# Two small elementwise operations of an attention stage move from VectorE to GpSimd

## The chip, the cores and the metric

The kernel runs on 1 core of one Trainium2 chip. The metric is the device time of one execution in microseconds (us), as the median of several runs. The profiled execution has a span as well, from its first to its last instruction; all rows below are read from that one execution.

## The reference

One transformer block on x of shape (2, 2048, 512), in float32, conditioned by a vector per batch. What matters here is the attention, with 16 heads of width 32 and 2048 keys:

```python
attn = jnp.einsum('bhqd,bhkd->bhqk', q, k) * (1.0 / np.sqrt(hd))
attn = jax.nn.softmax(attn, axis=-1)
out = jnp.einsum('bhqk,bhkd->bhqd', attn, v)
out = out.transpose(0, 2, 1, 3).reshape(B, T, C)
return out @ w_ao + b_ao
```

Before it come the conditioning, a normalisation and the projection to q, k and v with rotation; after it the output projection, a second normalisation and a gated feed-forward layer.

## The kernel before

The kernel is a sequence of stages: `stage_p` (conditioning), `stage_a` (q, k, v), `stage_b` (attention), `stage_c` (output projection and second normalisation) and `stage_d`, called twice (feed-forward). Only `stage_b` is touched. It lies between about 500 us and 2480 us of the span.

**Units.** Attention is done in 32 units (`UNITS`). A unit is a group of 4 heads (`GH`) of one batch and a block of 512 queries (`TB`); each group of heads has 4 units, and the first of them (`j % 4 == 0`) also sets off the load of the keys and values of the next group (`load_group`, 4 MB). They are called the loading units here. Within a unit `kt` runs over 16 tiles of 128 keys. The index u of the code counts so that the output work of unit u - 1 is done while unit u is computed.

**One step of kt.** TensorE works through a written-out order: `ORDER[kt]` says where the score matmuls (`s`, L805), the matmuls for the row maxima of a later unit (`m`, L780), the denominator matmuls (`d`, L810) and the transposition of the maxima (`t`, L799) stand. The order of a plain step is "smsdmmsms", of which the `d` is taken only at kt 0, 2 and 13, and it is followed by four matmuls of probabilities by values (L870, recorded as eight), here called the PV block. At kt 12 the order is "smsdmsmst". ScalarE takes the exponential of each of the four score tiles (L651) into one of four slots of the ring `pt`. VectorE reduces each of the four `m` tiles to a maximum (L714). A score matmul waits until the exponential two tiles earlier is done (`LEAD = 2`), an `m` matmul until the reduction four tiles earlier is done (`EARLY = 4`). Each engine works strictly in the order of its own program, and waits with its semaphores where it stands.

**Denominators.** The probabilities are added over kt. GpSimd adds the tiles of `BY_POOL` (kt 0, 1, 2, 4, 5, 7, 8, 10, 11, 13, 14; ten additions L686 of 128x2048), sends those of `BY_DMA` (kt 3, 6, 9) into `side` by accumulating DMAs (L693, L697), and adds `side` itself after kt 11 (L701, `SIDE_AT`). The rest goes to TensorE. Before ScalarE writes a slot of the ring again, `slot_free` waits until the adder of its old tile is done with it. The sums are ready when GpSimd has done its last addition (kt 14), and TensorE needs them at kt 2 of the next unit.

**The output of the unit before.** ScalarE copies the products (`read_products`, L623, after two exponentials of kt 0) and the denominators (`read_denominators`, L627, after kt 2) to memory that all can read. SyncE spreads the denominators over the partitions by DMAs, VectorE inverts them (`invert`, L728, at kt 4), and four DMAs bring the reciprocals back as `r_sb`. Then come the three steps around the change:

- `divide`, L732: `on` = `o_sb` * `r_sb`, 128x512, on VectorE after its reductions of kt 8
- `round_output`, L632: `o_hi` = `on` rounded, on ScalarE after its exponentials of kt 9; it waits for `on_ready`
- `split_output`, L736: `o_lo` = `on` - `o_hi`, on VectorE after its reductions of kt 10; it waits for `ohi_ready`

SyncE stores both (`store_output`, L571), and only behind them in its queue come the maxima of the next unit (`load_maxima`, L564 and L566), which TensorE needs for the first score of the next unit, issued in kt 15. `read_products` of the next unit waits for `olo_ready` too. The instruction that holds ScalarE's place is

```python
def round_output(u):
    act.wait_ge(on_ready, u + 1)
    act.wait_ge(o_stored, 32 * (u + 1))
    act.activation(o_hi[:], on[:], ACT.Copy).then_inc(ohi_ready, 1)
```

The functions in full, with the line numbers of the profile:

Of the kernel before, what the change touches and what calls it, by code (L numbers as in the profile page):

```python
# [17 lines left out]
ALU = mybir.AluOpType  # L18
# [11 lines left out]
GH = P // HD  # L30
NG = NB * H // GH
NK = T // P
UNITS = NG * NJ
# [9 lines left out]
def f32(ap):  # L43
    return ap.bitcast(F32)
# [431 lines left out]
def stage_b(nc, io, keep, scratch):  # L476
# [9 lines left out]
    with ExitStack() as stack:  # L486
# [15 lines left out]
        o_sb, d_sb, r_sb, on = (m.sb(n, [P, TB]) for n in ("o_sb", "d_sb", "r_sb", "on"))  # L502
        dcol = m.sb("dcol", [P, GH * TB // P])
        o_hi, o_lo = m.sb("o_hi", [P, TB], F32R), m.sb("o_lo", [P, TB], F32R)
# [22 lines left out]
        def added(kt):  # L527

            return max(BY_POOL.index(kt), 1) + (kt > SIDE_AT)
# [11 lines left out]
        def run(eng, body):  # L541
            with eng.Fori(0, UNITS // 8) as pair:
                for j in range(8):
                    body(8 * pair + j, pair, j)
# [120 lines left out]
        @block.gpsimd  # L665
        def _(pool):
            pool.memset(one_rows, 1.0).then_inc(ones_ready, 1)

            pool.memset(acc[1][:], 1.0).then_inc(ones_ready, 1)
            pool.wait_ge(ones_in, 32)  # L670
            pool.memset(pt[:, RING - 1, :, :], 1.0).then_inc(ones_ready, 1)
            pool.sem_inc(pool_added, NPOOL)

            def body(u, pair, j):
                sums = acc[j % 2]
                for kt in range(1, NK):
                    if kt in BY_POOL:
                        n = added(kt) - 1
                        pool.wait_ge(p_ready, STEPS * (u + 1) + GH * (kt + 1))
                        if n == 0:  # L680
                            pool.wait_ge(d_ps, u + 1)
                            a = pt[:, BY_POOL[0] % RING, :, :]
                        else:
                            pool.wait_ge(pool_added, NPOOL * (u + 1) + n)
                            a = sums[:]
                        pool.tensor_tensor(sums[:], a, pt[:, kt % RING, :, :], ALU.add).then_inc(pool_added, 1)  # L686
                    elif kt in BY_DMA:
                        n = BY_DMA.index(kt)
                        pool.wait_ge(p_ready, STEPS * (u + 1) + GH * (kt + 1))
                        if n == 0:  # L690
                            pool.wait_ge(pool_added, NPOOL * (u + 1) + added(kt - 1))
                            pool.nop(nofuse=True)
                            pool.dma_start(side[:], pt[:, kt % RING, :, :]).then_inc(side_in, 16)  # L693
                        else:
                            pool.wait_ge(side_in, 16 * (len(BY_DMA) * u + n))
                            pool.nop(nofuse=True)
                            pool.dma_start(side[:], pt[:, kt % RING, :, :], accum_op=ALU.add).then_inc(side_in, 16)  # L697
                    if kt == SIDE_AT:
                        pool.wait_ge(side_in, 16 * len(BY_DMA) * (u + 1))
                        pool.wait_ge(pool_added, NPOOL * (u + 1) + added(kt))  # L700
                        pool.tensor_tensor(sums[:], sums[:], side[:], ALU.add).then_inc(pool_added, 1)  # L701

            run(pool, body)

        @block.vector
        def _(dve):
            dve.sem_inc(max_done, ITEMS)
            dve.sem_inc(olo_ready, 1)
            dve.sem_inc(mlo_ready, 1)

            def maxima(n, slot, lo, hi):
                for i in range(lo, hi):
                    dve.wait_ge(max_ps, ITEMS * n + i + 1)
                    dve.tensor_reduce(mpart[slot][:, i // 4, i % 4:i % 4 + 1], ps_m[:, i % EARLY, :], AX.X, ALU.max).then_inc(max_done, 1)  # L714

            def finish_max(n, slot):
                dve.wait_ge(max_done, ITEMS * (n + 2))
                dve.tensor_reduce(mneg[:], mpart[slot][:], AX.X, ALU.max, negate=True).then_inc(mneg_ready, 1)

            def split_max(n):  # L720
                dve.wait_ge(mT_ps, n + 1)
                dve.tensor_copy(m_hi[:], ps_m[0:GH * SUB, EARLY - 1, 0:P]).then_inc(mhi_ready, 1)
                dve.wait_ge(mhi_ready, n + 1)
                dve.tensor_tensor(m_lo[:], ps_m[0:GH * SUB, EARLY - 1, 0:P], f32(m_hi[:]), ALU.subtract).then_inc(mlo_ready, 1)

            def invert(u):
                dve.wait_ge(dcol_in, 16 * (u + 1))
                dve.reciprocal(dcol[:], dcol[:]).then_inc(recip, 1)  # L728

            def divide(u):  # L730
                dve.wait_ge(r_in, 16 * GH * (u + 1))
                dve.tensor_tensor(on[:], o_sb[:], r_sb[:], ALU.mult).then_inc(on_ready, 1)  # L732

            def split_output(u):
                dve.wait_ge(ohi_ready, u + 1)
                dve.tensor_tensor(o_lo[:], on[:], f32(o_hi[:]), ALU.subtract).then_inc(olo_ready, 1)  # L736

            maxima(0, 0, 0, ITEMS)
            finish_max(0, 0)
            maxima(1, 1, 0, PLAN[TURN])  # L740
            split_max(0)
            maxima(1, 1, PLAN[TURN], AHEAD)

            def body(u, pair, j):
                at = AHEAD
                for kt in range(NK):
                    if kt == TURN:
                        finish_max(u + 1, (j + 1) % 2)
                        at = 0
                    ahead = 1 if kt < TURN else 2  # L750
                    maxima(u + ahead, (j + ahead) % 2, at, at + PLAN[kt])
                    at += PLAN[kt]
                    if kt == TURN:
                        split_max(u + 1)
                    if kt == 4:
                        invert(u)
                    if kt == 8:
                        divide(u)
                    if kt == 10:
                        split_output(u)  # L760

            run(dve, body)
            invert(UNITS)
            divide(UNITS)
            split_output(UNITS)

        @block.tensor
        def _(pe):
# [502 lines left out]
def build(nc, io, out):  # L1271

    scratch = {}
    for name, shape in (("qk_hi", (2, NG, P, T)), ("qk_lo", (2, NG, P, T)), ("v", (NG, P, NK, P)), ("o_hi", (NG, P, T)),
                        ("o_lo", (NG, P, T)), ("h_hi", (NG, P, T)), ("h_lo", (NG, P, T)), ("y0", (NB, T, D)),
                        ("y1", (NB, T, D)), ("m", (2, 2, GH * TB)), ("d", (2, GH, TB))):
        scratch[name] = nc.dram_tensor(f"scratch_{name}", shape, F32, kind="Internal").ap()
    with ExitStack() as whole:
        m = Memory(nc, whole, "keep")
        keep = {"chan": m.sb("chan", [P, C_ALL]), "cond_ab": m.sb("cond_ab", [P, NB, 4, KT]),  # L1280
                "ident": m.sb("ident", [P, P]), "ones": m.sb("ones", [P, P]),
                "bao": m.sb("bao", [P, D]), "bfo": m.sb("bfo", [P, D]),
                "w_ao": m.sb("w_ao", [P, KT, D])}
        with ExitStack() as early:
            m = Memory(nc, early, "early")
            keep |= {"w_hi": m.sb("w_hi", [P, KT, 3 * D], F32R), "w_lo": m.sb("w_lo", [P, KT, 3 * D], F32R),
                     "cos": m.sb("cos", [P, T]), "sin": m.sb("sin", [P, T]), "bv": m.sb("bv", [P, D]),
                     "x": m.sb("x", [P, SUB, D])}
            stage_p(nc, io, keep)
            stage_a(nc, io, keep, scratch)  # L1290
        nc.disable_value_cache = True
        stage_b(nc, io, keep, scratch)
        nc.disable_value_cache = False
        stage_c(nc, io, keep, scratch)
        for half in range(2):
            stage_d(nc, io, keep, scratch, out, half)
# [37 lines left out]
```

## Time and profile before

| | |
|---|---|
| median of 3 runs | 3795.44 us (3787.93 to 3796.56) |
| the profiled execution, its own time | 3794.34 us |
| its span | 3792.4 us |
| TensorE matmul busy, share of the span | 3380.3 us, 89% |
| VectorE busy | 2198.2 us, 58% |
| ScalarE busy | 1592.5 us, 42% |
| GpSimd busy | 1929.7 us, 51% |

PE is TensorE, DVE is VectorE, ACT is ScalarE, POOL is GpSimd and SP is SyncE. The shares are averages over stages with different limits: GpSimd's lies almost all in `stage_b`. An engine's row in a timeline gives start, duration, line, operation, output and inputs, count, and in square brackets how long the engine sat idle before it and what ended the wait. Several instructions in a row are merged into one row with a count.

### The profile page before, as it was taken

To read this page: it belongs to the slowest core of one execution; us is meant where nothing else is said; L and a number is where in the kernel's file an instruction comes from. 1 tells how busy PE (TensorE), PEld (TensorE's weight loads), DVE (VectorE), ACT (ScalarE), POOL (GpSimd) and SP (SyncE) were. 2 spreads that over 40 slices of the span, in tenths; PEclk is the share of its full clock that TensorE was granted. 3 is DMA by queue.
4 is the path that set the end of the run, shared out by engine and by line. 5 is a ranking of instruction groups with operands and counts; after the bars stand their busy time and mean duration, and the time that the engine had idled before them with its cause. 6 is when DMAs were issued, how large, how long until landed. Compare 5 with 4: busy or idle time off the path is not lost. (4 is left out here: it accounts for less than half of the span.)

```text
span 3792.4 us, 53992 instructions
## 1 busy us (share of the span) xinstructions
PE 3380.3 (89%) x15699; PEld 2105.7 (56%) x15699; DVE 2198.2 (58%) x3311; ACT 1592.5 (42%) x2851; POOL 1929.7 (51%) x634
## 2 busy tenths in 40 slices
PE   6888689999899998998989989956499999799999
PEld 5666444444344443443434444445388888688887
DVE  2878577877688786787777877835322222322212
ACT  1343136656566565565656656623311111211111
POOL 0222248988799898888888888944200000100000
PEclk9999779999999999998999999977699999899999
DMA  4444532343533434334334352367422120331120
GB/s 173 141 141 141 140 95 74 92 117 77 122 77 93 113 85 116 83 84 116 86 87 114 74 135 73 80 235 245 141 97 89 44 86 14 122 106 49 59 74 23
DMA packets 168123, 389.98 MB, mean 103 GB/s; under 512 B 23946, under 2 KB 41466, under 8 KB 150142
## 3 DMA queue, kind: packets, MB, share of 16 engines
q1 hardware_dynamic: 139700, 250.89, 22.4%
q0 software_dynamic: 17664, 113.26, 12.1%
q10 hardware_dynamic: 10512, 22.81, 1.8%
q8 instruction: 122, 2.00, 0.2%
q14 instruction: 125, 1.02, 0.1%
HBM read 183.83 MB, written 102.27 MB: 75 GB/s over the span
## 5 line engine op out<-in xcount | busy, mean ns | idle before, releaser
L714 DVE TENSOR_REDUCE b_mpart<-b_m 128x1 f32<-128x512 f32 x2127 | 1326.8, 683 | 416.1 <-PE b_m L780 415.0
L651 ACT ACTIVATE b_pt<-b_s 128x512 f32<-128x512 f32 x2048 | 1123.7, 595 | 775.5 <-PE b_s L805 723.1
L686 POOL TENSOR_TENSOR b_acc<-b_acc,b_pt 128x2048 f32<-128x2048 f32 x288 | 1355.4, 4706 | 54.7 <-ACT b_pt L651 39.6
L780 PE MATMUL b_m<-b_ks,b_qs 96*128 96x512 f32 x2127 | 816.9, 430 | 140.6 <-DVE b_mpart L714 116.2
L805 PE MATMUL b_s<-b_qs,b_ks 98*128 98x512 f32 x2050 | 905.0, 442 | 28.9 <-issue 17.1
L805 PEld LDWEIGHTS b_s<-b_qs,b_ks 98*128 98x128 f32 x2050 | 400.2, 195 | 658.0 <-ACT b_pt L651 544.6
L780 PEld LDWEIGHTS b_m<-b_ks,b_qs 96*128 96x128 f32 x2127 | 416.7, 200 | 322.1 <-DVE b_mpart L714 246.3
L870 PE MATMUL b_o<-b_pt,b_vg 128*32 128x512 f32 x4096 | 575.6, 635 | 0.0
L1210 DVE SCALAR_TENSOR_TENSOR d_uf<-d_a,keep_chan,d_sg 128x512 f32<-128x512 f32 x128 | 96.1, 751 | 578.2 <-PE d_a L1238 578.2
L1162 POOL DMA_DIRECT2D d_raw<-in_w_fc x32 | 23.9, 754 | 591.4 <-POOLq L1087 495.7
L1181 ACT ACTIVATE d_sg<-d_g,keep_chan 128x512 f32<-128x512 f32 x128 | 88.0, 688 | 418.7 <-PE d_g L1238 418.7
L1184 ACT ACTIVATE d_u_hi<-d_uf 128x512 fp32r<-128x512 f32 x128 | 80.9, 632 | 435.1 <-DVE d_uf L1210 435.1
L342 POOL TENSOR_TENSOR a_qc<-a_q,early_cos 128x512 f32<-128x512 f32 x64 | 92.3, 1442 | 325.9 <-ACT a_q L308 295.1
L686 POOL TENSOR_TENSOR b_acc<-b_pt 128x2048 f32<-128x2048 f32 x32 | 146.3, 4573 | 184.9 <-ACT b_pt L651 184.9
L1238 PE MATMUL d_g<-d_h_hi,d_w_hi 128*128 128x512 f32 x512 | 201.4, 393 | 43.6 <-DVE d_w_lo L1199 43.6
L1238 PE MATMUL d_g<-d_h_lo,d_w_hi 128*128 128x512 f32 x512 | 201.1, 393 | 0.0
L1238 PE MATMUL d_g<-d_h_hi,d_w_lo 128*128 128x512 f32 x512 | 201.1, 393 | 0.0
L1238 PE MATMUL d_a<-d_h_hi,d_w_hi 128*128 128x512 f32 x512 | 199.6, 390 | 0.0
L1238 PE MATMUL d_a<-d_h_lo,d_w_hi 128*128 128x512 f32 x512 | 199.5, 390 | 0.0
L1238 PE MATMUL d_a<-d_h_hi,d_w_lo 128*128 128x512 f32 x512 | 199.2, 389 | 0.0
L1251 PE MATMUL d_y<-d_w_hi,d_u_lo 128*128 128x512 f32 x512 | 199.2, 389 | 0.0
L1251 PE MATMUL d_y<-d_w_hi,d_u_hi 128*128 128x512 f32 x512 | 199.2, 389 | 0.0
(133 smaller groups left out, 3880.8 us busy)
## 6 DMA issues: line engine op xcount, KB each, us to landing
b_side<-b_pt POOLq DMA_DIRECT2D x96, 1024.0 KB, 7.0
b_ks<-scratch_qk_hi SPq DMA_DIRECT2D x18, 1024.0 KB, 14.2
b_qs<-scratch_qk_hi SPq DMA_DIRECT2D x68, 256.0 KB, 4.4
scratch_qk_hi<-a_q_hi SPq DMA_DIRECT2D x64, 256.0 KB, 2.5
scratch_qk_lo<-a_q_lo SPq DMA_DIRECT2D x64, 256.0 KB, 2.8
d_h_hi<-scratch_h_hi SPq DMA_DIRECT2D x16, 1024.0 KB, 7.4
d_h_lo<-scratch_h_lo SPq DMA_DIRECT2D x16, 1024.0 KB, 9.6
d_y<-scratch_y SPq DMA_DIRECT2D x16, 1024.0 KB, 8.0
```

Of the source, the lines that this page charges most:

```text
L342: pool.tensor_tensor(qc[:, t % 2, :], q[:, t % 2, :], cos[:, bass.ds(it * TB, TB)], ALU.mult).then_inc(qc_ready, 1)
L651: act.activation(pt[:, kt % RING, h, :], ps_s[:, i % LEAD, :], ACT.Exp, scale=SCALE).then_inc(p_ready, 1)
L686: pool.tensor_tensor(sums[:], a, pt[:, kt % RING, :, :], ALU.add).then_inc(pool_added, 1)
L714: dve.tensor_reduce(mpart[slot][:, i // 4, i % 4:i % 4 + 1], ps_m[:, i % EARLY, :], AX.X, ALU.max).then_inc(max_done, 1)
L780: pe.matmul(ps_m[:, i % EARLY, :], qs[qslot][0:KR, h, s * P:(s + 1) * P], ks[kslot][0:KR, h, k * TB:(k + 1) * TB], start=True, stop=True). ...
L805: pe.matmul(ps_s[:, i % LEAD, :], ks[kslot][0:QR, h, kt * P:(kt + 1) * P], qs[qslot][0:QR, h, :], start=True, stop=True).then_inc(st_done, 1)
L870: last = pe.matmul(ps_o[h * HD:(h + 1) * HD, 0, :], vg[kslot][:, kt, h * HD:(h + 1) * HD], pt[:, kt % RING, h, :], start=kt == 0, stop=kt ...
L1181: act.activation(sg[:, f % 2, :], ps_g[:, f % 2, :], ACT.Silu, bias=chan[:, t:t + 1]).then_inc(sg_ready, 1)
L1184: act.activation(u_hi[:, f % 2, :], uf[:, f % 2, :], ACT.Copy).then_inc(uhi_ready, 1)
L1210: dve.scalar_tensor_tensor(uf[:, f % 2, :], ps_a[:, f % 2, :], chan[:, t:t + 1], sg[:, f % 2, :], ALU.add, ALU.mult).then_inc(uf_ready, 1)
L1238: last = pe.matmul(ps[:, f % 2, :], w[:, f, t, k, :], h[s][:, k, :], start=i == 0, stop=i == 3 * KT - 1)
L1251: last = pe.matmul(ps_y[:, i, :], u[:, f % 2, i * P:(i + 1) * P], w[:, f, :], start=f == 0 and n == 0, stop=f == NF - 1 and n == 2)
```

## The change

GpSimd now does `divide` and `split_output`. `divide` stands behind its addition for kt 8 and ahead of the DMA for kt 9; `split_output` stands behind its addition for kt 11 and ahead of the addition of `side`. VectorE does neither any more. `round_output` keeps its place on ScalarE, behind the exponentials of kt 9. After the last unit both run on GpSimd too. The first credit of `olo_ready` is given by GpSimd. Nothing else changes.

```diff
@@ block.gpsimd
             pool.sem_inc(pool_added, NPOOL)
+            pool.sem_inc(olo_ready, 1)
+
+            def divide(u):
+                pool.wait_ge(r_in, 16 * GH * (u + 1))
+                pool.tensor_tensor(on[:], o_sb[:], r_sb[:], ALU.mult).then_inc(on_ready, 1)
+
+            def split_output(u):
+                pool.wait_ge(ohi_ready, u + 1)
+                pool.tensor_tensor(o_lo[:], on[:], f32(o_hi[:]), ALU.subtract).then_inc(olo_ready, 1)
...
+                    if kt == 8:
+                        divide(u)
+                    if kt == 11:
+                        split_output(u)
                     if kt == SIDE_AT:
...
             run(pool, body)
+            divide(UNITS)
+            split_output(UNITS)
@@ block.vector
-            dve.sem_inc(olo_ready, 1)
...
-            def divide(u):
-                dve.wait_ge(r_in, 16 * GH * (u + 1))
-                dve.tensor_tensor(on[:], o_sb[:], r_sb[:], ALU.mult).then_inc(on_ready, 1)
-
-            def split_output(u):
-                dve.wait_ge(ohi_ready, u + 1)
-                dve.tensor_tensor(o_lo[:], on[:], f32(o_hi[:]), ALU.subtract).then_inc(olo_ready, 1)
...
-                    if kt == 8:
-                        divide(u)
-                    if kt == 10:
-                        split_output(u)
 
             run(dve, body)
             invert(UNITS)
-            divide(UNITS)
-            split_output(UNITS)
```

## Rows read from the trace of the kernel before

**Rows 1.** The page: busy time, share of the span and instructions of each engine.
```profile
PE 3380.3 (89%) x15699; PEld 2105.7 (56%) x15699; DVE 2198.2 (58%) x3311; ACT 1592.5 (42%) x2851; POOL 1929.7 (51%) x634
```
**Rows 2.** Timeline of TensorE in an ordinary unit: start, duration, engine, line.
```profile
1135.37 1.06 PE L810 MATMUL b_d<-b_acc,keep_ones 128*32 128x512 f32 x8
...
1143.94 1.07 PE L870 MATMUL b_o<-b_pt,b_vg 128*32 128x512 f32 x8
...
1147.04 1.06 PE L870 MATMUL b_o<-b_pt,b_vg 128*32 128x512 f32 x8
...
1160.52 0.51 PE L805 MATMUL b_s<-b_qs,b_ks 98*128 98x512 f32 x1
...
1165.74 1.06 PE L870 MATMUL b_o<-b_pt,b_vg 128*32 128x512 f32 x8
...
1169.95 0.70 PE L780 MATMUL b_m<-b_ks,b_qs 96*128 96x512 f32 x1 [2.73 <-DVE b_mpart L714]
...
1177.44 1.07 PE L870 MATMUL b_o<-b_pt,b_vg 128*32 128x512 f32 x8
```
**Rows 3.** VectorE: the group of L736 over the span, then its timeline.
```profile
L736 DVE TENSOR_TENSOR b_o_lo<-b_on,b_o_hi x33: 692/4924/5608, 556.9 to 2477.9; 128x512 fp32r<-128x512 f32 x33
...
1157.42 1.48 DVE L732 TENSOR_TENSOR b_on<-b_o_sb,b_r_sb 128x512 f32<-128x512 f32 x1
...
1163.70 5.60 DVE L736 TENSOR_TENSOR b_o_lo<-b_on,b_o_hi 128x512 fp32r<-128x512 f32 x1
```
**Rows 4.** Timeline of GpSimd in the same unit, from its first addition to the next unit's.
```profile
1132.99 4.58 POOL L686 TENSOR_TENSOR b_acc<-b_pt 128x2048 f32<-128x2048 f32 x1 [2.88 <-ACT b_pt L651]
...
1153.47 9.87 POOL L686 TENSOR_TENSOR b_acc<-b_acc,b_pt 128x2048 f32<-128x2048 f32 x2
1163.28 0.87 POOL L697 DMA_DIRECT2D b_side<-b_pt  x1
...
1178.42 9.25 POOL L686 TENSOR_TENSOR b_acc<-b_acc,b_pt 128x2048 f32<-128x2048 f32 x2
1190.69 4.59 POOL L686 TENSOR_TENSOR b_acc<-b_pt 128x2048 f32<-128x2048 f32 x1 [3.02 <-ACT b_pt L651]
```
**Rows 5.** Timeline of GpSimd: the first additions of two units that follow each other.
```profile
643.05 4.58 POOL L686 TENSOR_TENSOR b_acc<-b_pt 128x2048 f32<-128x2048 f32 x1 [3.59 <-ACT b_pt L651]
...
701.28 4.57 POOL L686 TENSOR_TENSOR b_acc<-b_pt 128x2048 f32<-128x2048 f32 x1 [3.54 <-ACT b_pt L651]
```
**Rows 6.** Products and sums of 128x512 on GpSimd, in stages a and c.
```profile
L342 POOL TENSOR_TENSOR a_qc<-a_q,early_cos x64: 1285/1410/1752, 86.2 to 418.2; 128x512 f32<-128x512 f32 x64
...
2492.74 5.01 POOL L956 TENSOR_TENSOR c_x<-c_x,keep_bao 128x512 f32<-128x512 f32 x4 [26.59 <-DMA c_x<-in_x]
```
**Rows 7.** Timeline of ScalarE in the unit of Rows 2.
```profile
1159.03 0.63 ACT L632 ACTIVATE b_o_hi<-b_on 128x512 fp32r<-128x512 f32 x1
```
**Rows 8.** A loading unit: ScalarE's and GpSimd's timelines.
```profile
1531.76 0.63 ACT L632 ACTIVATE b_o_hi<-b_on 128x512 fp32r<-128x512 f32 x1
...
1525.77 9.69 POOL L686 TENSOR_TENSOR b_acc<-b_acc,b_pt 128x2048 f32<-128x2048 f32 x2 [4.28 <-ACT b_pt L651]
```
**Rows 9.** The same loading unit: TensorE's timeline where it had waited.
```profile
1518.17 0.76 PE L780 MATMUL b_m<-b_ks,b_qs 96*128 96x512 f32 x1 [4.83 <-DVE b_mpart L714]
...
1542.09 0.79 PE L780 MATMUL b_m<-b_ks,b_qs 96*128 96x512 f32 x1 [2.04 <-DVE b_mpart L714]
```
**Rows 10.** Windows of 10 us behind waits: us, PE busy, PEclk, DMA share, GB/s.
```profile
1518.17:1528.17 10.00, 10.00 (x35) 0.66 0.64 134
2008.93:2018.93 10.00, 10.00 (x43) 0.79 0.64 133
1542.09:1552.09 10.00, 10.00 (x39) 0.66 0.09 31
1054.73:1064.73 10.00, 9.30 (x46) 1.00 0.09 31
```
**Rows 11.** Timeline of SyncE's queue in the unit of Rows 2.
```profile
1175.79 0.23 SPq L566 DMA_DIRECT2D b_qs<-scratch_m  x1
```

## The prediction

> **What bounds the kernel now.** I read the page's busy shares first: TensorE is busy for 89% of the span [rows 1], but a share is an average over stages, so I went on to the timelines of the stage that is changed, engine by engine, over one ordinary unit.
>
> TensorE sets the pace. A plain step of kt lasts 3.10 us from PV block to PV block (1143.94 to 1147.04, [rows 2]). One stretch of the unit stands out. From the PV block of kt 11 (1165.74) to that of kt 13 (1177.44) 11.70 us pass. Two plain steps, the denominator block of kt 13 (1.06, [rows 2]), less one `m` (about a quarter of a microsecond) and plus the short transposition, come to 3.10 + 3.10 + 1.06 - 0.1 = 7.2 us. So 4.5 us are lost there. 2.73 us of them are TensorE idle for VectorE's reductions [rows 2], and the rest is mostly a granted clock below full speed afterwards.
>
> The reason stands on VectorE. `split_output` takes 4.92 us in the median of 33, up to 5.61, where its last one, after GpSimd's work has ended, takes 0.69 [rows 3]. In this unit it begins at 1163.70, just when a pair of GpSimd additions runs, and the reductions queue behind it. `divide` takes 1.48 us [rows 3]. The pair of additions that lies across it takes 9.87 us where the last pair of the unit takes 9.25 [rows 4]. Two-input work of both engines on SBUF is evidently in each other's way.
>
> The Trainium skill agrees with this row (GPSIMD Engine Reference, Specifications): GpSimd's SBUF interfaces are shared with VectorE and contend with VectorE instructions that have two SBUF inputs. By that rule alone the change could only help; it is rival B below.
>
> GpSimd is nearly full. From the unit's first addition (1132.99) to the end of its last (1187.67) it is almost without a gap, and it sits idle for 3.02 us before the next unit's, waiting for ScalarE [rows 4]. The ordinary unit lasts 57.7 us here [rows 4] and 58.2 typically [rows 5]. Without the loss at kt 12 TensorE would need 57.7 - 4.5 = 53.2 us.
>
> **The change, part by part.**
>
> *VectorE loses two operations.* The 5.60 us of `split_output` and the 1.48 us of `divide` go. `divide` cost TensorE nothing visible: no wait of TensorE follows it, the reductions catch up in the next two steps. With `split_output` the whole loss goes: 4.5 us in the unit of the rows, and 58.2 - 53.2 = 5.0 us in a typical one.
>
> *GpSimd gains two.* The nearest rows are a 128x512 addition at 5.01 / 4 = 1.25 us and products between 1.29 and 1.75 us, the latter beside VectorE's work [rows 6]. I take 1.25, and 1.75 as the upper end; below 1.1 there is no row, since a quarter of 4.58 [rows 4] is 1.15. The additions also lose the hindrance by VectorE, 9.87 - 9.25 = 0.6 us for each of two pairs. GpSimd would need, from its first addition to its last: 29.7 us to the end of the addition of kt 8 (1163.34 - 0.6 - 1132.99), then 1.3 for `divide` with its gap, 23.8 for the rest (1187.67 - 1163.28 = 24.4, less 0.6), and 1.3 for `split_output`: 56.1 us at most. That alone fits in the 58.2 us of now.
>
> The Trainium skill speaks against moving elementwise work in general (GPSIMD Engine Reference, Engine selection): two-input operations are about twice as slow on GpSimd, because two operands share one read port. The rows give 1.25 against 0.69 us; here the price of the operation itself is small beside the waits around it.
>
> *The order of ScalarE.* This is the step that decides. `round_output` stands behind the exponentials of kt 9 and waits for `on`. It now starts at 1159.03 without a wait [rows 7]. GpSimd's `divide` stands behind its addition of kt 8, which ends at 1163.34 with VectorE's hindrance and at about 1162.7 without [rows 4]. The quotient is ready at 1162.7 + 0.05 + 1.25 = 1164.0. So ScalarE stands still for 1164.0 - 1159.0 = 5.0 us. Behind it in its queue are the exponentials of kt 10 and all later ones. The first score matmul that TensorE issues in kt 10 (1160.52, [rows 2]) needs the first of these, so TensorE stops as well, with the `m` matmuls behind it in its order. It already waits there for about as long as `round_output` takes, and I give it 0.1 us of slack: 4.9 us of TensorE.
>
> The wait can't be escaped by GpSimd running better. The additions of kt 7 and 8 can't begin before the exponentials of kt 7 are done; they take 9.25 us, the quotient 1.25; ScalarE comes to `round_output` two steps after kt 7, 6.2 us. That leaves at least 10.5 - 6.2 = 4.3 us at full speed of TensorE. A loading unit shows about that case: the pair starts at 1525.77 after a wait and would end near 1535.0 without VectorE's `divide` in it (9.69 against 9.25), plus 1.3 is 1536.3, against 1531.76 of ScalarE: 4.5 us [rows 8], 4.4 of TensorE.
>
> *The clock after the wait.* TensorE's granted clock is below full speed in the 10 us behind a wait of such length. At 1518.17, behind 4.83 us idle, it is 0.66 [rows 9, 10]. The eight waits of VectorE for the denominators, one in each loading unit, with TensorE idle for 4.1 to 6.8 us, show 0.65 to 0.79, mean 0.70. The clock's two levels are 1.2 and 2.4 GHz, so a mean of 0.70 over 10 us costs 10 x 0.30 = 3.0 us (2.1 to 3.5).
>
> *After the wait* GpSimd has caught up and itself waits for the exponentials of kt 10, ready some 3.5 us after the quotient. It is then done with kt 14 about 59 us after its start (29.7 + 1.3 + 3.5 + 24.5), ahead of TensorE's 61, so it does not set the pace.
>
> *SyncE.* The store of `o_lo` stands ahead of `load_maxima`. `split_output` would end at about 45 us after the unit's first addition; the maxima, produced at kt 12, are ready at about the same time. The load of them was issued at 1175.79 [rows 11], 42.8 us after the start, and becomes about 47.5. TensorE needs it in kt 15, some 52 us after the start. I cost it at nothing; the cover is 2 to 3 us.
>
> *The end of the stage.* Both operations stand on the path after the last unit: 2 x (1.25 - 0.69) = 1.1 us. The moved credit of `olo_ready` costs nothing: it is given long before the first use.
>
> **The sum.** An ordinary unit: 53.2 + 4.9 + 3.0 = 61.1 us against 58.2, +2.9. There are 24: +70 us. A loading unit loses 4.4 + 3.0 = 7.4 us at the new wait, against what it loses at kt 12 now: 2.04 idle [rows 9], and a clock of 0.66 in some and 1.00 in others [rows 10]: 2.0 + 3.4 = 5.4 at most, and not below 2.0. I take 4.9 for it, near the ordinary unit's 5.0, since most are of the first kind: +2.5, eight times: +20 us. With the end +91 us. On the profiled execution's 3794.3 us this gives 3885, and the median of runs lies 1 us above it: 3886 us.
>
> **The rivals.**
>
> *A, my forecast:* a wait of ScalarE for GpSimd takes the place of VectorE's stall, and costs more. Its own range: wait 4.3 to 5.5 us (`divide` at 1.75), clock loss 1.7 to 3.4, which gives units of 59.1 to 62.0 us, +30 to +120 us: 3825 to 3915.
>
> *B, faster:* the stall of VectorE goes, and the new wait is hidden. Then GpSimd is the bound at 56 us a unit, or less. 32 x (58.2 - 56) = 70 us: 3725. For it speaks that VectorE's stall is real and goes. Against it, that the quotient comes 5 us after ScalarE is ready to take it; B needs it by 1159.0. If the wait and its clock loss together stay below 5.0 us, the kernel is faster, and if the wait is 4.3 that leaves 0.7 for the clock.
>
> *C, no change:* the wait comes, but the clock is kept, as behind the 2.04 us of idle at 1054.73 [rows 10]: 53.2 + 4.9 = 58.1 against 58.2. Then 3790 to 3800. Against it: all eight waits above 4 us cost clock.
>
> *D, slower still:* SyncE's chain loses its cover, because `split_output` waits behind GpSimd's addition of kt 11, and the first score of the next unit waits for the maxima. With 1 to 2 us a unit on top of A: 3915 to 3950.
>
> **How the numbers follow.** A 0.74, B 0.09, C 0.06, D 0.11. 0.3% of 3795 us, about what a measurement of this kernel can tell from no change, is 11 us. Slower holds A and D, a little less for the tail of A: 0.84. Faster is B: 0.09. Within 0.3%: 0.07. The range leaves out B, C and the upper half of D: 3815 to 3925 us.
>
> **What would show it.** In the profile after, `round_output` has idle time before it, ended by POOL `on`, of about 4.5 to 5 us in each of 32 units (some 155 us in all), and TensorE's first score of kt 10 shows as much. The waits of TensorE for VectorE at kt 12 are gone, the eight of the loading units stay. The two GpSimd operations take 1.2 to 1.4 us. The ordinary unit is 61 us. I am wrong if `round_output` starts without a wait, if the operations take far more than 1.75 us, if the granted clock after the wait stays near 1, or if TensorE waits for the maxima in kt 15.

## The result

The changed kernel takes 3883.79 us in the median of 4 runs (3878.75 to 3888.42), against 3793.72 us before (also 4 runs, 3787.93 to 3796.56): a ratio of 1.0238, 95% interval 1.0221 to 1.0254. It is slower by 90 us, or 2.4%. The profiled execution took 3888.42 us, with a span of 3886.6 us.

The page first, with the busy shares. Beside [rows 1] VectorE has lost 185 us of busy time and GpSimd gained only 55 us; by sums of work this would look like a good trade.

```profile
PE 3405.1 (88%) x15699; PEld 2136.9 (55%) x15699; DVE 2012.9 (52%) x3245; ACT 1590.7 (41%) x2851; POOL 1985.1 (51%) x700
```

The list of waits within the attention stage (engine and line that waited, what it waited for: us in total, times, longest) shows where the time is:

```profile
ACT b_o_hi L632 <- POOL b_on L677: 164.1, 32, 5.3
PE b_s L805 <- ACT b_pt L651: 151.8, 32, 5.0
...
PE b_m L780 <- DVE b_mpart L728: 44.1, 8, 8.1
```

ScalarE's rounding waits in each of the 32 units for GpSimd's quotient, 5.1 us on average, and TensorE waits behind it, 4.7 us on average. TensorE's waits for VectorE's reductions are down to the eight of the loading units; the one at kt 12 [rows 2] is gone.

The timeline of ScalarE in an ordinary unit of the changed kernel, to be read beside [rows 7]:

```profile
617.66 0.63 ACT L632 ACTIVATE b_o_hi<-b_on 128x512 fp32r<-128x512 f32 x1 [5.34 <-POOL b_on L677]
```

GpSimd in the same unit, beside [rows 4]:

```profile
586.34 4.58 POOL L695 TENSOR_TENSOR b_acc<-b_pt 128x2048 f32<-128x2048 f32 x1 [1.35 <-ACT b_pt L651]
...
606.83 9.48 POOL L695 TENSOR_TENSOR b_acc<-b_acc,b_pt 128x2048 f32<-128x2048 f32 x2
616.27 1.25 POOL L677 TENSOR_TENSOR b_on<-b_o_sb,b_r_sb 128x512 f32<-128x512 f32 x1
...
621.31 4.54 POOL L695 TENSOR_TENSOR b_acc<-b_acc,b_pt 128x2048 f32<-128x2048 f32 x1 [2.98 <-ACT b_pt L651]
...
631.16 1.28 POOL L681 TENSOR_TENSOR b_o_lo<-b_on,b_o_hi 128x512 fp32r<-128x512 f32 x1
...
647.64 4.58 POOL L695 TENSOR_TENSOR b_acc<-b_pt 128x2048 f32<-128x2048 f32 x1 [1.35 <-ACT b_pt L651]
```

The operations themselves cost 1.25 and 1.28 us. The quotient can't start before the pair of additions for kt 7 and 8 ends, at about 616.3; ScalarE has been ready since 612.3 and waits 5.3 us, 4.0 for the additions and the rest for the quotient. From first addition to first addition the unit lasts 61.3 us. GpSimd waits itself for 2.98 us behind the quotient, since ScalarE's stall has stopped the exponentials that it needs.

And TensorE, beside [rows 2], with a window of 10 us behind its wait:

```profile
612.80 1.06 PE L870 MATMUL b_o<-b_pt,b_vg 128*32 128x512 f32 x8
...
618.83 0.79 PE L805 MATMUL b_s<-b_qs,b_ks 98*128 98x512 f32 x1 [4.96 <-ACT b_pt L651]
...
626.93 1.07 PE L870 MATMUL b_o<-b_pt,b_vg 128*32 128x512 f32 x8
...
634.39 1.07 PE L870 MATMUL b_o<-b_pt,b_vg 128*32 128x512 f32 x8
```

```profile
618.83:628.83 10.00, 10.00 (x36) 5.29 (x36) 5.50 (x10) 5.47 (x10) 6.75 (x2) 0.67 0.59 131
```

From the PV block of kt 9 (612.80) to that of kt 11 (626.93) 14.13 us pass where two plain steps take 6.2: 7.9 us lost, 4.96 idle and the rest at the lower clock (granted clock 0.67 in the ten microseconds behind the wait). From kt 11 to kt 13 it is 7.46 us instead of 11.70.

### The profile page after: what moved, and what is told of

It is laid out like the page before. It is cut to its first block and busy times, and to the rows that moved or that the text cites. A ratio compares the mean times of both kernels' runs of the same rounds, so it can differ in the third digit from the quotient of the medians.

```text
span 3886.6 us, 53992 instructions
## 1 busy us (share of the span) xinstructions
PE 3405.1 (88%) x15699; PEld 2136.9 (55%) x15699; DVE 2012.9 (52%) x3245; ACT 1590.7 (41%) x2851; POOL 1985.1 (51%) x700
## 5 line engine op out<-in xcount | busy, mean ns | idle before, releaser
L695 POOL TENSOR_TENSOR b_acc<-b_acc,b_pt 128x2048 f32<-128x2048 f32 x288 | 1322.0, 4590 | 167.6 <-ACT b_pt L651 154.7
L805 PE MATMUL b_s<-b_qs,b_ks 98*128 98x512 f32 x2050 | 930.0, 454 | 168.8 <-ACT b_pt L651 152.1
L780 PE MATMUL b_m<-b_ks,b_qs 96*128 96x512 f32 x2127 | 830.5, 437 | 66.8 <-DVE b_mpart L728 44.1
L805 PEld LDWEIGHTS b_s<-b_qs,b_ks 98*128 98x128 f32 x2050 | 412.8, 201 | 807.4 <-ACT b_pt L651 687.6
L780 PEld LDWEIGHTS b_m<-b_ks,b_qs 96*128 96x128 f32 x2127 | 433.0, 207 | 231.0 <-DVE b_mpart L728 150.5
L1251 PE MATMUL d_y<-d_w_lo,d_u_hi 128*128 128x512 f32 x512 | 199.2, 389 | 0.0
```

The lines of the kernel that those rows point to most:

```text
L780: pe.matmul(ps_m[:, i % EARLY, :], qs[qslot][0:KR, h, s * P:(s + 1) * P], ks[kslot][0:KR, h, k * TB:(k + 1) * TB], start=True, stop=True). ...
L805: pe.matmul(ps_s[:, i % LEAD, :], ks[kslot][0:QR, h, kt * P:(kt + 1) * P], qs[qslot][0:QR, h, :], start=True, stop=True).then_inc(st_done, 1)
L1251: last = pe.matmul(ps_y[:, i, :], u[:, f % 2, i * P:(i + 1) * P], w[:, f, :], start=f == 0 and n == 0, stop=f == NF - 1 and n == 2)
```

## The experiments

Two theories were put to the test. *The wait theory*: the cost is ScalarE standing still at `round_output`, because GpSimd's quotient comes behind two long additions. *The rival*: the cost is GpSimd's added work as such, on an engine that was nearly full. All ratios are to the kernel before, on the same chip. Its own median there lies between 3790.35 and 3798.46 us, so the medians of runs on different chips can be compared to some 8 us only; for smaller differences the ratios are the ones to read.

| run | edit | median, us | ratio, 95% interval |
|---|---|---|---|
| the changed kernel | | 3883.79 | 1.0238 [1.0221, 1.0254] |
| e1 | rounding at kt 11 | 3760.61 | 0.9923 [0.9907, 0.9940] |
| e2 | rounding at kt 10 | 3748.21 | 0.9882 [0.9865, 0.9898] |
| e3 | remainder alone moved | 3713.83 | 0.9796 [0.9779, 0.9812] |
| e4 | quotient alone moved | 3886.52 | 1.0253 [1.0235, 1.0270] |
| e5 | spare product ahead of the quotient | 3907.45 | 1.0299 [1.0275, 1.0323] |
| e6 | spare product behind the remainder | 3884.37 | 1.0240 [1.0222, 1.0258] |
| e7 | before, remainder of 32 columns | 3764.93 | 0.9928 [0.9908, 0.9948] |
| e8 | quotient at kt 7 | 3734.55 | 0.9850 [0.9825, 0.9876] |
| e9 | e1 with the quotient behind the DMA | 3737.01 | 0.9846 [0.9822, 0.9870] |
| e10 | e3 with the rounding at kt 10 | 3715.20 | 0.9792 [0.9770, 0.9814] |
| e11 | before, without the remainder | 3701.54 | 0.9752 [0.9731, 0.9772] |

### e1 and e2: the same work, another place of the wait

```diff
-                    if kt == 9:
+                    if kt == 11:
                         round_output(u)
```

> The changed kernel, with ScalarE's rounding of the output behind the exponentials of kt 11 instead of kt 9. GpSimd's work is the same to the instruction. If ScalarE's wait for the quotient is the cost, the wait goes (the quotient is ready about 31 us after the unit's first addition, ScalarE comes to it at about 32), GpSimd becomes the bound at 29.9 + 11.2 + 15.1 = 56.2 us a unit plus a short start, and the kernel takes 3715 to 3750 us. If the rival is right that GpSimd's added work as such is the cost, it stays within 1% of 3884 us.

e2 has `kt == 10` in the same place.

> The changed kernel, with the rounding behind the exponentials of kt 10. The wait theory: ScalarE comes 3.1 us later to it, so of its wait of 5.1 us 2.0 stay in each unit. With TensorE idle 1.9 us and a clock loss of 0 to 2 us the unit takes 57 to 58 us: 3740 to 3785 us. GpSimd's work as the cost: within 1% of 3884 us.

GpSimd's instructions are the same in these and in the changed kernel. Moving one line of ScalarE by one step takes 136 us off the changed kernel, and by two steps 123 us. In e2 ScalarE's rounding still waits, as expected; in e1 only once, after the last unit:

```profile
ACT b_o_hi L632 <- POOL b_on L677: 63.0, 32, 9.8
```

Less the last, that is 1.7 us a unit, beside 5.1. The rival, which asked for no change in either, falls with these two runs. But e1, with the longer reprieve, is slower than e2 and missed its range by 11 us. Its list of waits has a large new entry, a wait of ScalarE for a slot of the ring that a DMA is still reading:

```profile
ACT b_pt L651 <- DMA b_side<-b_pt: 120.8, 54, 4.0
```

In the timeline of e1 the DMA of kt 9 is issued at 669.14, behind the quotient; at kt 13 ScalarE stands still until 677.26:

```profile
667.91 1.28 POOL L677 TENSOR_TENSOR b_on<-b_o_sb,b_r_sb 128x512 f32<-128x512 f32 x1
669.14 0.86 POOL L706 DMA_DIRECT2D b_side<-b_pt  x1
```

```profile
677.26 2.28 ACT L651 ACTIVATE b_pt<-b_s 128x512 f32<-128x512 f32 x4 [3.92 <-DMA b_side<-b_pt]
```

### e9: the DMA behind the quotient

e1, with the quotient one place later on GpSimd:

```diff
-                    if kt == 8:
+                    if kt == 9:
                         divide(u)
```

> The kernel with the rounding at kt 11, but with GpSimd's quotient behind the DMA of kt 9 instead of ahead of it. In the run with the quotient ahead, ScalarE waited up to 4.0 us at kt 13 for that DMA (issued at 669.14, landed after 8 us). If the DMA put off by the quotient is what that run lacked of its 3715 to 3750 us, it is now issued 1.2 us earlier, ScalarE's wait for it falls from 121 us in all to about 80 us, and the kernel takes 3730 to 3750 us. If it is something else, 3761 us stay.

3737.01 us: 24 us less than e1 (29 by the ratios, for the two ran on different chips), with the same work and the same place of the rounding. ScalarE's waits for the DMA fall from 120.8 to 88.9 us. So a good part of what e1 lacked was the DMA that the quotient put off. That is a second price of `divide` at this place. In the changed kernel ScalarE has no such wait; I take it to be hidden behind the longer stall, which no run tests.

### e3, e4 and e10: one part alone

```diff
@@ block.gpsimd (e3)
-                    if kt == 8:
-                        divide(u)
                     if kt == 11:
                         split_output(u)
@@ block.vector (e3)
+                    if kt == 8:
+                        divide(u)
```

> One part of the change alone: the remainder is GpSimd's (behind its addition of kt 11), the quotient stays VectorE's at kt 8. The wait theory: ScalarE doesn't wait, VectorE's stall at kt 10 is gone, GpSimd is the bound at some 55.5 us a unit (one hindered pair, +0.6, one operation less, -1.3, against 56.2): 3690 to 3735 us. GpSimd's added work as the cost: about half of the change's loss, 3840 us. If VectorE's remainder was no cost at all before, 3795 us.

e4 is the mirror image: `divide` on GpSimd at kt 8, `split_output` on VectorE at kt 10.

> The other part alone: the quotient is GpSimd's, the remainder stays VectorE's at kt 10. The wait theory: ScalarE's wait of about 5 us stays in each unit, and VectorE's remainder, now just ahead of GpSimd's addition of kt 10, is held up as well for up to 4.6 us: 3900 to 4000 us. GpSimd's added work as the cost: about half of the change's loss, 3840 us.

e3 is 2.0% faster than the kernel before (3713.83 against 3790.35 us), the best, with e10, of all versions that compute everything. e4 is as slow as the whole change. So the whole loss sits in the moved quotient. The moved remainder is a gain of 77 us where the quotient stays on VectorE, but it is hardly to be seen where the quotient is moved (3 us, e4 against the changed kernel): the effects of the two parts don't simply add up. The rival, which gave each part half of the loss, is wrong for both.

The rows of GpSimd in e3 point to its new bound. Ahead of the first addition there is no idle time any more in 23 of 31 units, and the ordinary unit lasts 55.4 us in the median, 55.3 us here:

```profile
636.80 4.58 POOL L691 TENSOR_TENSOR b_acc<-b_pt 128x2048 f32<-128x2048 f32 x1
...
692.13 4.56 POOL L691 TENSOR_TENSOR b_acc<-b_pt 128x2048 f32<-128x2048 f32 x1
```

e4 missed its range on the fast side: I expected VectorE's stalled remainder to be paid on top. It does stall, but at almost no cost:

```profile
621.99 3.58 DVE L739 TENSOR_TENSOR b_o_lo<-b_on,b_o_hi 128x512 fp32r<-128x512 f32 x1
```

The ordinary unit lasts 61.4 us, against 61.2 in the changed kernel. The wait of TensorE in kt 10 is the same in both (4.95 us), the lower clock in the 10 us behind it costs less in e4 (2.6 us against 3.2), and about 0.7 us are lost elsewhere. Why the clock was kinder there was not tested.

e10 tries for more with e3 and the rounding at kt 10.

> The kernel with only the remainder on GpSimd, with ScalarE's rounding one step later (kt 10), to try for more. ScalarE's small waits for VectorE's quotient (20 us in all) go. If GpSimd's row of additions without a gap (55.3 us a unit) is the bound there, nothing is won: 3705 to 3720 us. If ScalarE is part of the bound, some 3695 us.

3715.20 against 3713.83 us: nothing is won. ScalarE's waits for the quotient are gone but for the last one, and its waits for the side DMAs have grown from 66.3 to 95.5 us. So the small waits did not bound e3.

### e5 and e6: the same added work in two places

```diff
+                        pool.tensor_tensor(spare[:, 1, :], spare[:, 0, :], spare[:, 0, :], ALU.mult)
```

On the changed kernel, ahead of `divide` in e5, behind `split_output` in e6.

> The changed kernel with one more 128x512 product on GpSimd (1.27 us, of a spare tile with itself, used by nothing) ahead of its quotient in every unit. The wait theory: ScalarE's wait grows from 5.1 to 6.4 us and TensorE loses it in full: 32 x 1.3 = +41 us on the changed kernel, 3915 to 3935 us. GpSimd's work as the cost: the same here as in the kernel with the product behind the remainder.

> The same additional product, but behind the remainder. Nobody waits for it. The wait theory: it fits in the 1.35 us that GpSimd sits idle ahead of the next unit's first addition, so the kernel stays at 3884 us, up to 3892. GpSimd's work as the cost: +41 us, as with the product ahead of the quotient.

e6 costs nothing (3884.37 against 3883.79 us); e5 costs 24 us. The same operation on the same engine is free in one place and not in the other, which only the wait theory gives. GpSimd's idle time ahead of the next unit shrinks in e6 from 1.35 to 0.30 us:

```profile
645.34 4.58 POOL L697 TENSOR_TENSOR b_acc<-b_pt 128x2048 f32<-128x2048 f32 x1 [0.30 <-ACT b_pt L652]
```

The size of e5 was off: 24 us instead of 41, and 8 us below its range. One part is that the spare product takes 1.03 us, not 1.27. The waits grow by that: ScalarE's rounding from 173.7 to 204.5 us with the last one (33 waits), TensorE's first score of kt 10 from 151.8 to 182.7 us (32 waits), 0.97 us each. The loading unit grows by more than that, 1.35 us on average, but the ordinary unit only by 0.5 us, from 61.2 to 61.7. There about half of the added wait comes back from the clock: the granted clock of the ten microseconds behind the wait is 0.68 on average over the ordinary units of the changed kernel and 0.74 in e5, which is 3.2 and 2.6 us lost (over all 32 waits 0.685 and 0.730). During the wait itself it is lower in e5, 0.84 against 0.94.

Slow time inside the wait costs TensorE nothing. Counted as length times what the clock lacks of full speed, wait and ten microseconds together have 3.5 us of it in the ordinary units of the changed kernel and 3.6 in e5; 0.3 and 1.0 of it lie in the wait. But the length of the wait is not what decides this: e4 has the wait of the changed kernel, 4.95 us, and 3.5 us of slow time as well, with 0.9 inside the wait. So e5 shows what the clock gave back there, and no price for a longer wait in general.

### e8: the quotient one addition earlier

```diff
-                    if kt == 8:
+                    if kt == 7:
                         divide(u)
```

> The changed kernel with GpSimd's quotient behind its addition of kt 7 instead of kt 8, the rounding at kt 9 as in the changed kernel. The wait theory: the quotient is ready at about 26.6 us after the unit's first addition, ScalarE comes to it at 26.1: a wait of 0.5 us is left. GpSimd is the bound at 56.2 us, and with the DMA of kt 9 as late as in the changed kernel some wait of ScalarE for its slot: 3735 to 3765 us. GpSimd's work as the cost: within 1% of 3884 us.

3734.55 us, at the edge of what was expected. ScalarE's rounding waits for 31.4 us in all, 25 times, the 9.8 us after the last unit among them. This is the changed kernel with the quotient and one addition exchanged in GpSimd's order, and it is 1.5% faster than the kernel before instead of 2.4% slower.

### e7 and e11: what VectorE's remainder cost before

e7, on the kernel before (of the remainder, 480 of 512 columns are left out):

```diff
+            dve.memset(f32(o_lo[:]), 0.0)
...
-                dve.tensor_tensor(o_lo[:], on[:], f32(o_hi[:]), ALU.subtract).then_inc(olo_ready, 1)
+                dve.tensor_tensor(o_lo[:, 0:32], on[:, 0:32], f32(o_hi[:, 0:32]), ALU.subtract).then_inc(olo_ready, 1)
```

> The kernel before, but VectorE computes only 32 of the 512 columns of the remainder (the rest of it is left at zero, so that part of the computation is left out). If the operation waits for GpSimd's addition under way to end, it still takes 4.3 to 5.0 us (0.6 less than before) and the kernel 3765 to 3795 us. If the two engines only share bandwidth, it shrinks with its size to below 0.7 us, the stall of TensorE at kt 12 goes, and the kernel takes about 3700 us.

The group of the narrow remainder, durations in ns as smallest, median and largest:

```profile
L737 DVE TENSOR_TENSOR b_o_lo<-b_on,b_o_hi x33: 192/4456/5083, 558.6 to 2448.0; 128x32 fp32r<-128x32 f32 x33
```

With a sixteenth of the work it takes 4.46 us instead of 4.92 [rows 3]; the smallest, after GpSimd's work has ended, takes 0.19. It is a wait for the addition under way. In the timelines of both engines the remainder runs from 615.64 to 620.04, and the addition that began at 615.13 ends at 619.97:

```profile
615.64 4.40 DVE L737 TENSOR_TENSOR b_o_lo<-b_on,b_o_hi 128x32 fp32r<-128x32 f32 x1
```

```profile
615.13 4.84 POOL L686 TENSOR_TENSOR b_acc<-b_acc,b_pt 128x2048 f32<-128x2048 f32 x1
```

It is so in all 32 units: the narrow remainder ends 0.05 to 0.07 us behind an addition, and the full one of the kernel before 0.55 to 0.57 us behind. `divide` of the kernel before does the same in 30 of 32 units. In an ordinary one it begins 0.91 us ahead of the end of an addition and ends 0.57 us behind it, which makes its 1.48 us [rows 3]. In the other two it begins about 0.1 us ahead of an addition and takes 0.68 us, and the addition takes 5.0 us instead of 4.6. With 3764.93 us the kernel lies at the lower edge of what was expected.

The Trainium skill (SBUF — State Buffer, SBUF: two separate sides) says that the port pair the two engines share is an exclusive lock and not a split of bandwidth: whichever starts first holds it for its whole instruction. The rows agree that the wait lasts to the end of the addition. Who comes first they don't settle: in 14 of the 32 units of the kernel before, the recorded start of the remainder lies 0.13 to 0.19 us ahead of the addition's, and it waits all the same. The unit of [rows 3] is one of them, with the remainder recorded at 1163.70 and the addition of kt 10 at 1163.89:

```profile
1163.89 4.84 POOL L686 TENSOR_TENSOR b_acc<-b_acc,b_pt 128x2048 f32<-128x2048 f32 x1
```

e11 leaves the remainder out altogether.

```diff
-                dve.tensor_tensor(o_lo[:], on[:], f32(o_hi[:]), ALU.subtract).then_inc(olo_ready, 1)
+                dve.sem_inc(olo_ready, 1)
```

> The kernel before without VectorE's remainder: it is left out (o_lo stays zero), only its semaphore is raised. This is the whole price of VectorE's stall. TensorE alone would need 53.2 us a unit, GpSimd from first to last addition 54.1: about 54.2 us a unit against 58.2, 3660 to 3690 us. If the stall at kt 12 has another cause than the remainder, it stays at 3790 us.

3701.54 us, against 3798.46 us of the kernel before on the same chip: the remainder cost it some 95 us. I had expected 105 to 135. The ordinary unit is 55.0 us in the median, not 54.2, though TensorE waits for VectorE in the loading units alone; ScalarE now waits for the side DMAs, 72.5 us in all:

```profile
ACT b_pt L651 <- DMA b_side<-b_pt: 72.5, 50, 3.7
```

GpSimd is idle for some 0.6 us ahead of a unit's first addition. So TensorE's 53.2 us was not reached with the stall gone; the trace points to GpSimd and its DMAs as the bound, at about 55 us.

## Why the prediction was right

**VectorE's stall goes.** Right. The wait at kt 12 is gone from the list, and kt 11 to 13 takes 7.46 us, where I worked out 7.2. The cause was right too, and e7 makes it exact: I had written that the two engines are in each other's way, and the operation waits for the whole of the addition under way.

**The price of the two operations.** Right: 1.25 and 1.28 us, as the addition of stage c had it [rows 6].

**ScalarE's order decides.** Right, and the step on which the sign rests. I had 5.0 us of wait in an ordinary unit and 4.5 in a loading one; the mean of all is 5.1, and TensorE's idle time is 4.94 and about 4.15 (4.9 and 4.4 predicted). In the unit shown the wait is 5.3 us instead of 5.0, mostly because the pair of additions ahead of the quotient takes 9.48 us where I had 9.25. e1, e2 and e8 change the wait alone and turn the loss into a gain; e4 moves the quotient alone and has the whole loss.

**The clock.** Right in size for this wait: 0.685 over the 32 windows, 3.15 us, from 0.70 and 3.0 in [rows 10]. It can't be carried over to other kernels as a price of a wait: with waits of the same length e4 has 0.749, and e5, with longer ones, 0.730.

**The sum.** An ordinary unit was predicted at 53.2 + 4.9 + 3.0 = 61.1 us and is 61.2 on average, against 58.2 before. Its terms hold as well: 4.94 us of wait and 3.2 us of lower clock behind it leave 53.1. Twenty of them give 60 us. In three more, one at the end of every second group of heads, TensorE also stands still for 5 to 6 us, before and after the change, and the profile names nothing that it waits for; they grew by 3.8 us, 11 us in all. The loading units grew by 1.7 us instead of 2.5, 14 us in all. From the first addition of the last unit to the last remainder 7 us more pass, of which 1.2 are the end of the stage, predicted as 1.1. With 1.4 us that the stage begins later this makes 93 us, and the spans differ by 94.

In the loading units both prices were a little too high: the old stall cost 4.3 us (2.05 idle and 2.3 of clock), where I took 4.9, and the new one 7.1 (4.14 and 3.0), where I took 7.4. By these two the loading unit would have grown by 2.8 us. What I left out is the rest of the unit: the wait for the denominators was 0.2 us shorter, the clock behind it cost 2.5 instead of 3.0 us, and 0.4 us less was lost elsewhere. The errors of the loading units and of the others went in opposite ways and nearly cancelled, so that the total is met within 3 us is in part luck.

**GpSimd doesn't set the pace.** Right, with less room than I gave it: it is idle for 1.35 us ahead of the next unit, where I had 2, and e6 shows that the room is real. **SyncE** was right as well: the load of the maxima is issued 49.3 us after the unit's start (47.5 predicted, 42.8 before), and the list of waits has no wait of TensorE for it.

**The rivals.** B's time (3725) is near what the kernels reach in which the wait is gone or mostly hidden, 3714 to 3761 us; its condition, that the quotient be ready when ScalarE comes, was the right one. Its unit of 56 us is nearly what e8 has (56.2 us in the median of the ordinary units, 56.6 on average); ScalarE's waits for the side DMAs, 79.8 us in all in e8, were left out. C, the clock kept, did not occur: no window behind the 32 waits is above 0.83. D did not occur.

What stays open: how much of the rest of e9 above GpSimd's 56.2 us is owed to the store of `o_hi` beside the side DMA, and what decides how much of the slow time falls into a wait. Neither was tried.

## What to carry to other kernels

When work moves to another engine, ask where in that engine's queue it lands and who waits for its result in order. Here 1.25 us of work behind 9 us of additions cost 5 us of ScalarE and 8 us of TensorE a unit, and the same work one addition earlier cost some 20 us in all 32 units together (e8 against e3). Move the parts of a change one by one: one of these two alone makes the kernel 2.0% faster and the other alone 2.5% slower, and the best version is the one with the remainder alone moved (3714 us).

A two-input operation of VectorE that meets a long addition of GpSimd was priced here by what was left of the addition, not by its own size: 1.48 us for `divide`, which met its end, and 4.92 us for `split_output`, which met its start.

## What the runs showed of the hardware

- Of 512 columns or 32, VectorE's subtraction waits for GpSimd's 4.6 us addition to end: 4.92 and 4.46 us in the median, 0.69 and 0.19 us without GpSimd. In all 32 units it ends 0.55 to 0.57 us (narrow: 0.05 to 0.07 us) behind the addition.
- A product of a 128x512 tile with itself takes GpSimd 1.03 us, one of two tiles 1.26 us.
- Behind 32 waits of TensorE of 4.7 us on average the granted clock is 0.685 over the next 10 us in the changed kernel, and 0.749 in e4, where it was lower during the waits (0.85 against 0.93). Behind the 5.7 us waits of e5 it is 0.730, with 0.84 during the waits.
